# Two steps moved ahead in attention 1: the copy of sequence 2's normalised rows, and the projection of sequence 1's values

## The chip, the cores and the metric

The kernel runs on one core of a Trainium2 chip. The metric is the device time of one execution in microseconds (us). The core has engines that run side by side, each through its own list of instructions in order: PE (matmul, with PEld for its weight loads), DVE, ACT, POOL, and SP, which here only issues transfers (DMAs). They wait for each other through semaphores. A transfer is carried by 16 DMA engines; all transfers of this kernel are issued by SP on one queue.

## The reference

Two blocks of a transformer run over 8 sequences of 512 rows of 128 values: attention 0 (a linear attention), feed-forward 0 (with FP4 quantisation), attention 1 (causal softmax attention with 16 heads of 8), feed-forward 1 (a mixture of experts). Each is added to the input and has a normalisation ahead of it. The change touches the end of feed-forward 0 and the start of attention 1, which computes

```
def _L1_attn_ref(x, Wq, Wk, Wv, Wout):
    ...
    q = jnp.einsum('bld,dhe->blhe', x, Wq)
    k = jnp.einsum('bld,dhe->blhe', x, Wk)
    v = jnp.einsum('bld,dhe->blhe', x, Wv)
    a = jnp.einsum('bqhd,bkhd->bhqk', q, k) / Dh ** 0.5
    ...
    a = jnp.where(mask, a, NEG_INF)
    a = jax.nn.softmax(a, axis=-1)
    o = jnp.einsum('bhqk,bkhd->bqhd', a, v)
    return jnp.einsum('blhe,hed->bld', o, Wout)
x = x + _L1_attn_ref(_layernorm(x, axis=-1), L1_attn_Wq, L1_attn_Wk, L1_attn_Wv, L1_attn_Wout)
```

## The kernel before

The kernel is a row of four blocks, one after the other: `attention0`, `ffn0`, `attention1`, `ffn1`. Within a block each engine's work is written out in the order in which it runs; between two blocks all engines meet at a barrier (the branch at L858 is where they leave `ffn0`). Nothing reorders the instructions: the order of the text and the semaphores set everything.

**Attention 1** handles one sequence per period. A period has 20 steps (`STEPS`, four quads of heads with five units each). In a step of period i PE computes the scores of sequence i (`scores`, L1588), whose exponentials ACT takes (L1803) and POOL masks (L1865), and the scores of sequence i+1 once more in the other orientation (`maxima`, L1573 and L1577), from which DVE takes the row maxima (L1905, L1908, L1909, L1911). The two share three pairs of PSUM banks in turn (`ring`), so a matmul group waits until the group three places earlier was read. `weighted_v` (L1603) multiplies the exponentials with the values.

Ahead of period 0 stands the **opening**: 20 steps of `maxima` of sequence 0 alone, n = 0 to 19, in which a step n from 3 on waits until DVE has read unit n-3. Between these steps PE does small jobs that all use PSUM bank 0, so each waits for ACT's read of the one before:

- n = 0: `project_v(0, 0)` (L1630), the values of sequence 0; ACT keeps them (`keep_v`, L1778, semaphore `v_ready`);
- n = 2: `pr.turn_x(2)` (L782), which transposes the normalised rows of sequence 2. They are read from the buffer `xs`, into which SP copies them from `XN` (`pr.stage`, L754, semaphore `staged`). The copy is 256 KB;
- n = 4 and n = 6: `pr.project` (L787), the queries and keys of sequence 2; ACT keeps them (L798, `qf_ready`, `kf_ready`);
- n = 11: `turn_maxima(0, 0)` (L1637), which transposes the first half of the maxima of sequence 0, after DVE has split them (L1921 to L1924). ACT keeps them (L1784, `m_row`), and SP writes them to DRAM and back into `qS` (L1503, L1506). Period 0's first scores wait for that.

The values of sequence 1 are projected in period 0, step (1, 0), as those of each later sequence are in the period before their own. ACT keeps them there too.

**SP's part.** At the end of `ffn0` SP writes the split queries and keys of sequence 0 to DRAM (`parts_to_rows`, L763) and reads them back as rows of `qS` and `kS` (`pr.rows`, L777): 8 transfers of 192 KB. After the barrier its first transfer is `pr.stage(sp, 2)`, then the same two steps for sequence 1. `pr.stage(sp, n)` itself waits until `turn_x(n-1)` has read `xs`. ACT writes the normalised rows into `XN` in `norm_out` of `ffn0`, one sequence after the other, and counts them in `out_normed`.

## Time and profile before

| | us |
|---|---|
| median of 3 runs | 954.23 (954.03 to 956.84) |
| the profiled execution, its own time | 954.21 |
| its span, first to last instruction | 952.5 |
| end of `ffn0`, PE's first matmul of attention 1 | 378.11 |
| first scores of period 0 | 404.81 |

PE is busy for 872.2 us of the span, DVE for 737.9, ACT for 527.3, POOL for 453.6. The trace's instruction rows give the start, the duration, the engine, the line, and in brackets the idle time of the engine just before, with what ended it. "PEclk" or "granted clock" is the share of full speed that TensorE was given; 1.00 is 2.4 GHz and 0.50 is 1.2 GHz.

### The profile page before, as it was taken

To read this page: it belongs to the slowest core of one execution; us is meant where nothing else is said; L and a number is where in the kernel's file an instruction comes from. 1 tells how busy PE (TensorE), PEld (TensorE's weight loads), DVE (VectorE), ACT (ScalarE), POOL (GpSimd) and SP (SyncE) were. 2 spreads that over 40 slices of the span, in tenths; PEclk is the share of its full clock that TensorE was granted. 3 is DMA by queue.
4 is the path that set the end of the run, shared out by engine and by line. 5 is a ranking of instruction groups with operands and counts; after the bars stand their busy time and mean duration, and the time that the engine had idled before them with its cause. 6 is when DMAs were issued, how large, how long until landed. Compare 5 with 4: busy or idle time off the path is not lost. (4 is left out here: it accounts for less than half of the span.)

```text
span 952.5 us, 18274 instructions
## 1 busy us (share of the span) xinstructions
PE 872.2 (92%) x6457; PEld 577.6 (61%) x6457; DVE 737.9 (77%) x1496; ACT 527.3 (55%) x777; POOL 453.6 (48%) x599
## 2 busy tenths in 40 slices
PE   5999999998887777689999999998889999999997
PEld 4777777784665555344455454453557767766775
DVE  6888899878999995888888988987666646655542
ACT  4677778887465454267777777767523223222211
POOL 4123322324566665236566666456464355345344
PEclk9999999999999998779999999999999999999999
DMA  9200000000000007655445536200000000000000
GB/s 292 66 12 12 11 11 11 11 1 0 5 1 12 12 1 136 133 125 110 106 86 115 114 78 126 55 3 15 12 1 23 1 22 22 22 0 22 11 12 11
DMA packets 35641, 43.34 MB, mean 46 GB/s; under 512 B 4828, under 2 KB 27772, under 8 KB 35572
## 3 DMA queue, kind: packets, MB, share of 16 engines
q1 hardware_dynamic: 35569, 42.43, 18.6%
q8 instruction: 42, 0.69, 0.3%
q14 instruction: 30, 0.22, 0.1%
HBM read 21.21 MB, written 15.07 MB: 38 GB/s over the span
## 5 line engine op out<-in xcount | busy, mean ns | idle before, releaser
L1803 ACT ACTIVATE PT<-PS 128x1024 f32<-128x1024 f32 x160 | 162.7, 1023 | 56.5 <-PE PS L1588 56.2
L1865 POOL TENSOR_SCALAR_AFFINE_SELECT PT<-PT 128x256 f32<-128x256 f32 (+1 forms) x224 | 96.9, 448 | 109.6 <-ACT PT L1803 108.0
L2292 POOL TENSOR_TENSOR PRE_sb<-PRE_sb,VA 128x512 f32<-128x512 f32 x64 | 82.3, 1285 | 132.4 <-DVE PRE_sb L2360 132.3
L2258 ACT ACTIVATE sg_d<-PS 128x512 f32<-128x512 f32 x64 | 38.2, 597 | 160.0 <-PE PS L1326 160.0
L2360 DVE TENSOR_TENSOR PRE_sb<-sg_d,PS 128x512 f32<-128x512 f32 x64 | 44.0, 688 | 85.4 <-ACT sg_d L2258 84.7
L446 ACT ACTIVATE E<-PS,m 128x512 f32<-128x512 f32 x128 | 85.7, 687 | 36.8 <-PE PS L332 28.0
L1905 DVE TENSOR_REDUCE negm<-PS 128x2 f32<-128x1024 f32 x64 | 77.9, 1222 | 22.9 <-PE PS L1577 21.9
L1603 PE MATMUL PS<-PT,VA 128*32 128x512 f32 (+3 forms) x1024 | 89.5, 445 | 0.7 <-POOL PT L1865 0.7
L1573 PE MATMUL PS<-kS,qS 48*128 48x384 bf16 (+3 forms) x512 | 74.1, 314 | 8.1 <-ACT PT L1803 3.0
L491 POOL TENSOR_SCALAR Qs<-Qs 128x1024 f32<-128x1024 f32 x32 | 34.8, 1088 | 81.6 <-ACT Qs L427 81.0
L1908 DVE TENSOR_REDUCE negm<-PS 128x2 f32<-128x768 f32 x64 | 61.2, 957 | 12.8 <-PE PS L1577 11.5
L1588 PE MATMUL PS<-qS,kS 51*128 51x384 bf16 (+3 forms) x512 | 63.9, 308 | 2.9 <-DVE negm L1905 1.7
L360 PE MATMUL PS<-Qs,AW 128*128 128x512 f32 x128 | 59.2, 608 | 3.2 <-DVE PRE_sb L641 3.2
L1577 PEld LDWEIGHTS PS<-halves 64*128 64x128 bf16 x1024 | 48.9, 99 | 20.2 <-issue 2.9
L1588 PEld LDWEIGHTS PS<-qS,kS 51*128 51x128 bf16 x512 | 17.2, 94 | 69.6 <-issue 46.8
L1577 PE MATMUL PS<-halves 64*128 64x128 bf16 (+1 forms) x1024 | 58.8, 210 | 0.0
L422 ACT ACTIVATE Qs<-Qs,eps_c,ks 128x512 f32<-128x512 f32 x64 | 51.7, 814 | 0.0
L649 DVE SCALAR_TENSOR_TENSOR KB<-E,PS 128x512 f32<-128x512 f32 x64 | 42.3, 684 | 10.7 <-ACT E L446 9.0
L932 PE MATMUL PS<-low_space_sb,xT_sb 128*128 128x352 f32 x128 | 41.2, 465 | 9.1 <-DVE hh L1224 7.9
L670 DVE SCALAR_TENSOR_TENSOR Qs<-E,PS 128x512 f32<-128x512 f32 x64 | 42.6, 676 | 0.0
L664 DVE TENSOR_SCALAR E<-E 128x512 f32<-128x512 f32 x64 | 37.0, 579 | 6.8 <-ACT E L446 3.6
L2295 POOL TENSOR_TENSOR asum<-PRE_sb 128x512 f32<-128x512 f32 x32 | 41.0, 1282 | 2.5
(326 smaller groups left out, 2282.7 us busy)
## 6 DMA issues: line engine op xcount, KB each, us to landing
qk_rows<-parts SPq DMA_DIRECT2D x32, 192.0 KB, 2.8
qS<-qk_rows SPq DMA_DIRECT2D x32, 192.0 KB, 4.2
kS<-qk_rows SPq DMA_DIRECT2D x32, 192.0 KB, 4.6
xs_sb<-XN_sb SPq DMA_DIRECT2D x20, 256.0 KB, 2.3
qk_rows<-parts SPq DMA_DIRECT2D x32, 128.0 KB, 2.8
X_sb<-in_x_dram SPq DMA_DIRECT2D x8, 256.0 KB, 6.8
qk_rows<-parts SPq DMA_DIRECT2D x32, 64.0 KB, 2.5
out_dram<-X_sb SPq DMA_DIRECT2D x8, 256.0 KB, 2.3
```

Of the source, the lines that this page charges most:

```text
L360: ins = nc.tensor.matmul(PS[:, 6, :], AW[:, slot, c, :], Qs[:, slot, c, :], start=(c == 0), stop=(c == NC0 - 1))
L422: nc.scalar.activation(Qs[:, slot, c, :], Qs[:, slot, c, :], ACT.Ln, bias=eps_c[:, 0:1], scale=ks[:, c:c + 1]).then_inc(ln_ready, 1)
L446: nc.scalar.activation(E[:, u % RING, :], PS[:, RING_BANKS[u % RING], :], ACT.Exp, bias=m1[:, 0:1]).then_inc(e_ready, 1)
L1573: nc.tensor.matmul(bank[:, col:col + W], q[:, k * P:(k + 1) * P], key[:, 0:W], start=True, stop=False)
L1577: ins = nc.tensor.matmul(PS[:, 1 + 2 * ring_pair + j % 2, end - P + 64 * half:end], halves[rows, half, :], halves[rows, 2 + half, 64 * hal ...
L1588: ins = nc.tensor.matmul(PS[:, 1 + 2 * ring_pair + j % 2, col:col + W], key[:, kt * P:(kt + 1) * P], q[:, kt * P:S], start=True, stop=True)
L1603: ins = nc.tensor.matmul(PS[32 * j:32 * j + 32, 7, kt * P:S], VA[:, slot, kt, 4 * quad + j, :], PT[:, quad % 2, u, c:c + W], start=(kt == ...
L1803: nc.scalar.activation(PT[:, quad % 2, u, :], PS[:, b:b + 2, :].rearrange("p b n -> p (b n)"), ACT.Exp).then_inc(exp_ready, 1)
L1865: nc.gpsimd.affine_select(out=v, in_=v, pattern=[[0, 4 if u == 4 else 2], [1, P]], compare_op=ALU.is_ge, fill=0.0, base=0, channel_multipl ...
L1905: ins = nc.vector.tensor_reduce(negm[:, 3, :, 2 * quad + u], PS[:, b:b + 2, :], AX.X, ALU.max, negate=True)
L1908: nc.vector.tensor_reduce(negm[:, 2, :, pair], PS[:, b:b + 2, 0:384], AX.X, ALU.max, negate=True)
L2292: nc.gpsimd.tensor_tensor(acts[:, s, f, :], acts[:, s, f, :], W[:, slot, s, :], ALU.mult).then_inc(weighted, 1)
```

## The change

Four edits in three places:

- In `ffn0` SP issues `pr.stage(sp, 2)` after `pr.rows(sp, 0, 0, h)`, ahead of the barrier, behind a wait until `out_normed` is 3. In `attention1` the call is gone.
- In the opening PE projects the values of sequence 1 after step n = 8 (`project_v(1, 1)`), behind a wait for the kept keys of sequence 2 (`kf_ready` 3). ACT keeps the values there, behind the keys. `turn_maxima(0, 0)` at n = 11 now waits for these values (`v_ready` 2) instead of for the keys.
- In period 0 step (1, 0) has no projection of values any more, on PE and on ACT. The later periods keep theirs.
- In period 0 step (1, 3) `turn_ot(0, 0)` waits for `m_row` 2, where it waited for `v_ready` 2.

```diff
@@ ffn0, SP
             for h in range(NHALF):
                 pr.rows(sp, 0, 0, h)
-
+            sp.wait_ge(out_normed, 3)
+            pr.stage(sp, 2)
@@ attention1, SP
-            pr.stage(sp, 2)
             for m in range(2):
                 pr.parts_to_rows(sp, 1, 1, m)
@@ attention1, PE, period
-                    elif (quad, u) == (1, 0) and not (last or opens(i, 1)):
-                        if first:
-                            pe.wait_ge(m_row, 2)
-                        else:
-                            pe.wait_ge(o_normed, i * 4)
+                    elif (quad, u) == (1, 0) and not (first or last or opens(i, 1)):
+                        pe.wait_ge(o_normed, i * 4)
                         project_v(i + 1, 1 - slot)
...
                         if first:
-                            pe.wait_ge(v_ready, 2)
+                            pe.wait_ge(m_row, 2)
...
@@ attention1, PE, opening
+                elif n == 8:
+                    pe.wait_ge(kf_ready, 3)
+                    project_v(1, 1)
                 elif n == 11:
-                    pe.wait_ge(kf_ready, 3)
+                    pe.wait_ge(v_ready, 2)
                     pe.wait_ge(consts, 1)
                     turn_maxima(0, 0)
@@ attention1, ACT, period
-                    elif (quad, u) == ((1, 1) if opens(i, 1) else (1, 0)) and not last:
+                    elif (quad, u) == ((1, 1) if opens(i, 1) else (1, 0)) and not (first or last):
                         keep_v(i + 1, 1 - slot)
@@ attention1, ACT, opening
             pr.keep(act, 2, 1, k_ready, kf_ready)
+            keep_v(1, 1)
```

SP at the end of `ffn0`, before: the branches are the way out of `ffn0` and into `attention1`; L777 are the rows of sequence 0, L754 is the copy, L763 the parts of sequence 1.

```order
L777 DMA qS<-qk_rows 48x2048
L777 DMA kS<-qk_rows 48x2048
L858 UNCONDITIONAL_BRANCH
L1499 UNCONDITIONAL_BRANCH
L754 DMA xs_sb<-XN_sb 128x512
L763 DMA qk_rows<-parts 64x3x512
```

The same place after:

```order
L777 DMA qS<-qk_rows 48x2048
L777 DMA kS<-qk_rows 48x2048
L754 DMA xs_sb<-XN_sb 128x512
L858 UNCONDITIONAL_BRANCH
L1500 UNCONDITIONAL_BRANCH
L763 DMA qk_rows<-parts 64x3x512
```

The copy has moved ahead of the two branches, and still stands directly behind the last of the 8 row transfers, with no other transfer between them.

PE in the opening after, from the end of step n = 8 to step n = 9 (before, the L1630 row is not there and the others are the same):

```order
L1573 MATMUL PS<-kS,qS 128x128 x2
L1577 MATMUL PS<-halves 128x128 x2
L1577 MATMUL PS<-halves 128x64 x2
L1630 MATMUL PS<-wv1_sb,PRE_sb 128x128 x4
L1573 MATMUL PS<-kS,qS 128x256 x2
L1577 MATMUL PS<-halves 128x128 x2
```

PE in period 0, step (1, 0) and the start of step (1, 1), before:

```order
L1603 MATMUL PS<-PT,VA 32x512 x4
L1588 MATMUL PS<-qS,kS 128x512 x2
L1573 MATMUL PS<-kS,qS 128x512 x2
L1577 MATMUL PS<-halves 128x128 x2
L1577 MATMUL PS<-halves 128x64 x2
L1630 MATMUL PS<-wv1_sb,PRE_sb 128x128 x4
L1603 MATMUL PS<-PT,VA 32x384 x4
L1588 MATMUL PS<-qS,kS 128x512 x2
```

The same place after:

```order
L1603 MATMUL PS<-PT,VA 32x512 x4
L1588 MATMUL PS<-qS,kS 128x512 x2
L1573 MATMUL PS<-kS,qS 128x512 x2
L1577 MATMUL PS<-halves 128x128 x2
L1577 MATMUL PS<-halves 128x64 x2
L1603 MATMUL PS<-PT,VA 32x384 x4
L1588 MATMUL PS<-qS,kS 128x512 x2
```

The projection has left this place, and the weighted values (L1603) follow the maxima (L1577) directly.

## Rows read from the trace of the kernel before

**Rows 1.** The page's first part: busy us (share of the span), instructions.

```profile
PE 872.2 (92%) x6457; PEld 577.6 (61%) x6457; DVE 737.9 (77%) x1496; ACT 527.3 (55%) x777; POOL 453.6 (48%) x599
```

**Rows 2.** Timeline, PE, opening: start, us, engine, line, operation [idle before <-releaser].

```profile
384.13 0.63 PE L782 MATMUL PS<-ident_sb,xs_sb 128*128 128x128 f32 x4 [3.65 <-DMA xs_sb<-XN_sb]
...
390.71 0.25 PE L1577 MATMUL PS<-halves 64*128 64x128 bf16 x4
...
395.65 0.58 PE L1637 MATMUL PS<-identb,mpart 128*24 128x128 bf16 x4 [1.63 <-DVE mpart L1924]
```

**Rows 3.** Timeline, DVE, opening.

```profile
382.13 0.42 DVE L1909 TENSOR_REDUCE negm<-PS 128x2 f32<-128x256 f32 x1
385.38 0.96 DVE L1908 TENSOR_REDUCE negm<-PS 128x2 f32<-128x768 f32 x1 [2.83 <-PE PS L1577]
...
388.74 2.36 DVE L1905 TENSOR_REDUCE negm<-PS 128x2 f32<-128x1024 f32 x2 [0.94 <-PE PS L1577]
...
393.40 1.22 DVE L1911 TENSOR_REDUCE negm<-PS 128x4 f32<-128x1024 f32 x1
```

**Rows 4.** Timeline, ACT, opening.

```profile
380.60 0.60 ACT L1778 ACTIVATE VA<-PS 128x512 f32<-128x512 f32 x1
...
390.09 0.60 ACT L798 ACTIVATE PRE_sb<-PS 128x512 f32<-128x512 f32 x1 [1.37 <-PE PS L787]
```

**Rows 5.** Timeline, SP's queue, end of `ffn0` and opening: start and duration of the issue.

```profile
370.58 0.34 SPq L777 DMA_DIRECT2D qS<-qk_rows  x1
...
373.75 0.42 SPq L777 DMA_DIRECT2D kS<-qk_rows  x1
378.14 0.57 SPq L754 DMA_DIRECT2D xs_sb<-XN_sb  x1
...
393.99 0.42 SPq L777 DMA_DIRECT2D kS<-qk_rows  x1
396.88 0.30 SPq L1503 DMA_DIRECT2D max_rows<-mrow  x1
399.87 0.55 SPq L1506 DMA_DIRECT2D qS<-max_rows  x2
```

**Rows 6.** Transfers, KB, us from issue to landing: issued at 370.58, 373.75, 378.14.

```profile
qS<-qk_rows SPq DMA_DIRECT2D x1, 192.0 KB, 3.3
...
kS<-qk_rows SPq DMA_DIRECT2D x1, 192.0 KB, 8.4
...
xs_sb<-XN_sb SPq DMA_DIRECT2D x1, 256.0 KB, 5.9
```

**Rows 7.** Transfers, the same copy for sequence 0, issued at 330.38.

```profile
xs_sb<-XN_sb SPq DMA_DIRECT2D x1, 256.0 KB, 2.3
```

**Rows 8.** DMA queues, 380.8 to 384: packets, MB, share of 16 engines.

```profile
q8 instruction: 1, 0.02, 3.2%
```

**Rows 9.** Stretches: length, busy PE, PEld, DVE, ACT, POOL, clock, DMA share, GB/s.

```profile
372.00:381.00 9.00, 7.19 (x56) 5.23 (x54) 2.10 (x2) 6.21 (x12) 3.12 (x5) 0.84 1.04 173
...
382.40:383.60 1.20, 0.00 (x0) 0.00 (x0) 0.15 (x1) 0.03 (x1) 1.20 (x2) 1.00 0.06 14
...
385.00:388.40 3.40, 3.40 (x28) 1.37 (x24) 2.42 (x3) 0.67 (x2) 0.00 (x0) 0.51 0.95 203
...
395.40:415.80 20.40, 16.65 (x166) 8.16 (x168) 19.24 (x34) 8.54 (x11) 7.47 (x11) 0.50 0.73 153
...
409.10:415.40 6.30, 6.25 (x60) 2.89 (x60) 5.27 (x14) 3.61 (x4) 2.43 (x6) 0.50 0.91 200
```

**Rows 10.** Timeline, PE, period 0, step (1, 0).

```profile
416.20 1.16 PE L1630 MATMUL PS<-wv_sb,PRE_sb 128*128 128x128 f32 x8
417.29 0.85 PE L1603 MATMUL PS<-PT,VA 128*32 128x384 f32 x8
```

**Rows 11.** Timeline, DVE, after that step.

```profile
418.81 1.23 DVE L1905 TENSOR_REDUCE negm<-PS 128x2 f32<-128x1024 f32 x1 [1.27 <-PE PS L1577]
```

**Rows 12.** Timeline, ACT, after that step.

```profile
418.50 1.02 ACT L1803 ACTIVATE PT<-PS 128x1024 f32<-128x1024 f32 x1 [0.51 <-PE PS L1588]
```

## The prediction

> **What bounds the kernel now.** I first read the busy shares: PE has 872.2 us of work in a span of 952.5 us, 92% [rows 1]. So the kernel is bound by PE nearly everywhere, and a change gains only where PE's list gets shorter at a place where PE never waits, or where a wait of PE goes. The change touches two places, so I read the timeline engine by engine around each.
>
> In the opening of attention 1 PE does three steps and then stands for 3.65 us until the copy of sequence 2's rows has landed; its transposes start at 384.13 [rows 2]. This is the one long wait there. It passes to DVE, the engine that has the most work in the opening: it has read unit n = 2 by 382.55 (382.13 + 0.42), idles 2.83 us, then after the query projection another 0.94 us, and from 388.74 on runs without a pause [rows 3]. From there PE waits for DVE: 1.63 us before it transposes the split maxima at 395.65 [rows 2]. So in the opening DVE sets the pace, and a job added on PE there may cost nothing. In period 0 it is the other way round: at step (1, 0) PE has no idle time before its instructions [rows 10], while DVE idles 1.27 us and ACT 0.51 us until PE delivers [rows 11, 12].
>
> **The change part by part.** The sum is made against the profiled execution's own 954.21 us (the span and 1.7 us around it), which is within 0.02 us of the median, 954.23.
>
> *The copy, issued before the barrier.* SP issues the last row transfer at 373.75 (0.42 us), so the copy can be issued at about 374.2 instead of 378.14 [rows 5], 3.9 us earlier. Its two waits are for work that lies far back: `norm_out` is by then three sequences further than the third, and the transposes of sequence 1 have long read the buffer. SP otherwise only waits at the barrier until about 378, so the issue of 0.57 us delays nobody. The question is when the copy lands. The first of the 8 row transfers is issued at 370.58 and lands 3.3 us later, the last at 373.75 and lands 8.4 us later [rows 5, 6]: at 373.9 and 382.15. So 7 further transfers land in 8.25 us, one each 1.2 us, however fast SP issues them; it issued them within 3.2 us. They stand in line. The DMA engines were full from 372 to 381: share 1.04, 173 GB/s [rows 9]. The copy, issued at 378.14 and landing 5.9 us later, lands at 384.04, 1.9 us behind the last row transfer; the same copy with nothing ahead of it lands in 2.3 us [rows 6, 7]. It joined a line that lasted until 382.15, and stood directly behind the last row transfer. In the changed kernel it stands directly behind the same transfer, only longer. The line is as long, nothing that was behind the copy went ahead, and the last byte ahead of it moves when it did. So I take **0 us** for this move. It can't cost: rows for steps n = 10 on would have to be late by ten microseconds. Its other end is a landing before PE asks for it: then PE goes on when the values of sequence 0 are kept, at 381.20 (380.60 + 0.60) [rows 4], and DVE gets both idle times back, 2.83 + 0.94 = 3.77 us [rows 3]. I take the near end, because the row transfers show waiting in line directly.
>
> The Trainium skill (DMA: Bandwidth & Descriptors, Queues, rings and completion order) says that on each DMA engine descriptors are consumed in ring order. The landings one each 1.2 us agree with it; by that rule the earlier issue is worth nothing as long as the line never runs empty, and the whole change is worth the PE work alone. The same section says that completion is not in order per issuing engine; by that a gain up to the other end stays possible, and no row here shows it.
>
> What of the 1.9 us is not line? Once the share of the DMA engines has fallen, 0.06 is left from 382.4 to 383.6, that is one engine of 16 [rows 9], and in this stretch one instruction packet of another queue, which alone takes 3.2% of 16 engines over 3.2 us = 1.6 us of one engine, was carried [rows 8]. So a load of instructions held up one engine's part of the copy by about 1.2 to 1.4 us. It stays, since PE's and ACT's programs up to there are the same and reach it at the same time.
>
> *The projection of sequence 1's values, added after n = 8.* It takes 1.16 us at full clock [rows 10]. Step n = 8 ends at 390.96 (390.71 + 0.25), the keys are kept at 390.69 (390.09 + 0.60) [rows 2, 4], so PE starts it at once and ends near 392.1. Step n = 9 then starts near 392.1 and takes about 0.6 us, until 392.7. DVE takes that unit at 393.40 [rows 3]: 0.7 us to spare. Steps 10 and 11 wait for DVE as before. ACT's added 0.60 us falls into its idle time ahead of the maxima, and the new wait of `turn_maxima` (values kept near 392.8) is met 2.8 us before the split maxima are, near 395.6 [rows 2]. So **0 us**. The other end: if PE has the low clock there, the projection takes twice as long, 2.3 us, the cover of 0.7 us is used up and 0.5 us shows; uncovered altogether it would be 1.16 us.
>
> *The projection that period 0 no longer has.* The next instruction started at 417.29 against 416.20: **1.09 us** off a PE that never waits there [rows 10]. What would be late next? I followed the next steps with everything on PE 1.09 us earlier. DVE and ACT sat waiting for PE by 1.27 and 0.51 us [rows 11, 12]; ACT also loses its own 0.60 us keep there, and its next exponential was waiting for PE behind it. So both follow, DVE by the full 1.09 us, ACT likewise (0.51 + 0.60 = 1.11 us). The masks for the next weighted values are long done. After that each engine's distance to the others is as before, and since every later period is a chain of the same steps, the gain is carried to the end. Bounds: 0.5 us, if ACT followed by its idle time alone, and 1.16 us, the full duration.
>
> *The exchanged waits* at n = 11 and at (1, 3) are for things done microseconds earlier: 0 us.
>
> Sum: 0 + 0 - 1.09 = -1.1 us, 954.2 - 1.1 = **953.1 us**.
>
> **The rivals.**
>
> *A: as summed.* 953.1. To it belongs one variant of the clock. TensorE had 0.50 (1.2 GHz) from 395.4 to 415.8 [rows 9], after a stretch in which it mostly waited for DVE. The projection puts more matmuls ahead of that. Would the clock stay at 2.4 GHz, then little is won until 409, where DVE sets the pace, and of the 6.3 us from 409.1 to 415.4 no more than 6.3 - 5.27 = 1.0 us, since DVE is busy 5.27 us in it [rows 9]: 952.1. So A reaches from 951.9 to 954.3 with the spread of runs.
>
> *B: the copy lands early.* The line doesn't hold it, and PE's stall goes. For it: the copy has only 1.9 us of its own behind the line, and a stall of 3.65 us is the largest in the opening. Against it: the landings one each 1.2 us. Of the 3.77 us not all would last. Period 0 begins after the first half of the maxima went out to DRAM and back. SP sent them at 396.88 and could send them back in at 399.87, 3.0 us later; but it first issues rows of sequence 1 up to 394.41, and these hang on POOL's parts, not on the stall [rows 5]. So sending moves by 2.5 us at most and then stands behind the rows in line. Before, the way back had some 2 us to spare until 404.8. I take 3.3 us: 953.1 - 3.3 = 949.8, at most 949.3. A small relative: the copy lands before the load of instructions takes its engine, 1.3 us: 951.8.
>
> *C: slower, by the clock.* The low clock ended at 415.8, just before the projection of period 0 [rows 9, 10]. PE works without a pause there, and this mechanism takes the clock away for longer: dense f32 matmuls leave the place at which the clock had just come back, so it comes back later or falls again. The shortest low stretch of the opening is 3.4 us at 0.51 [rows 9]; PE at half speed loses half of it, 1.7 us: 953.1 + 1.7 = 954.8, and with two of them 956.5. It decides from 2.2 us of further low clock, which eat up the 1.09 us. Against it: the clock was back before the projection began, so what brought it back is still there. For it: the three runs of before already spread from 954.03 to 956.84.
>
> *D: the change doesn't do what it says.* The order of instructions shows that all four edits are there; the copy is issued earlier without landing earlier is A itself.
>
> **How the numbers follow.** A has a chance of 0.67, B 0.14, its relative at 951.8 0.06, C 0.13. The likeliest is A: 953.1. The range holds A, B and its relative and C's lower edge: 949.6 to 955.0. It leaves out the rest of C and the last bit of B, some 0.13. 0.3% is 2.9 us, about what a measurement of this kernel can tell from no change: faster means under 951.4, slower over 957.1. Faster is B with a little of the relative and of A's lower edge: 0.17. Slower by that much needs three low stretches: 0.03. Within: 0.80.
>
> **What would show it.** In the profile after: (1) the copy is issued near 374.2 and takes 9 to 10 us to land; PE's wait before the transposes is still 3 to 4 us and ends near 384. B is right if that wait is under 1 us and DVE's idle time of 2.83 us is gone. (2) L1630 stands near 391, DVE has no idle time before unit n = 9. (3) The first scores of period 0 start within 0.3 us of 404.8 after PE's start, measured from PE's first matmul: 26.7 us. (4) From step (1, 1) on everything is 1.1 us earlier than before. The prediction is wrong if the stall shrinks although the row transfers land as before, or if low-clock stretches lie elsewhere; then the clock's rows, not the steps, explain the difference.

## The result, and the profile after

| | before | after |
|---|---|---|
| median of 5 runs, us | 954.23 (952.78 to 956.84) | 949.82 (947.94 to 950.71) |
| ratio after / before, 95% interval | | 0.9949 [0.9931, 0.9966] |
| the profiled execution, its own time | 954.21 | 950.71 |
| its span | 952.5 | 949.0 |
| PE's first matmul of attention 1 | 378.11 | 378.33 |
| first scores of period 0 | 404.81 | 402.94 |

The change makes the kernel 4.4 us faster by these medians, where 1.1 us was predicted. A second series of 12 runs gave 0.9971 [0.9955, 0.9987] (below); over all 17 runs of after, and 72 of before in this and the next two series, the means are 951.1 and 954.5 us, 3.3 us apart. The forecast of 953.1 is wrong. The median came out where rival B (the copy lands early) had put it, 949.8; that is a coincidence, since the second series of the same kernel had 951.9 and what B described did not happen (below).

The page of after, first part: busy us (share of the span), instructions. It answers [rows 1].

```profile
PE 870.0 (92%) x6457; PEld 575.9 (61%) x6457; DVE 737.6 (78%) x1496; ACT 527.7 (56%) x777; POOL 454.0 (48%) x599
```

PE has 2.2 us less to do with the same number of instructions. No matmul was removed. The clock fits this: 1.2 GHz lasted 34 us of this execution and 42 us of the one of before (twice the span times what the mean granted clock, 0.982 and 0.978, lacks to 1). The prediction's sum has no term for it.

SP's queue of after, around the copy (start and duration of the issue), which answers [rows 5]:

```profile
371.60 0.34 SPq L777 DMA_DIRECT2D qS<-qk_rows  x1
...
374.76 0.42 SPq L777 DMA_DIRECT2D kS<-qk_rows  x1
375.31 0.57 SPq L754 DMA_DIRECT2D xs_sb<-XN_sb  x1
...
395.49 0.40 SPq L1504 DMA_DIRECT2D max_rows<-mrow  x1
400.22 0.55 SPq L1507 DMA_DIRECT2D qS<-max_rows  x2
```

Transfers of after, KB, us from issue to landing, for the last row transfer (issued at 374.76) and the copy (375.31), which answers [rows 6]:

```profile
xs_sb<-XN_sb SPq DMA_DIRECT2D x1, 256.0 KB, 7.9
kS<-qk_rows SPq DMA_DIRECT2D x1, 192.0 KB, 8.0
```

The row transfers are issued 1.0 us later than before, and the last one lands at 382.76. The copy lands at 383.21, **0.45 us behind it**. Before it landed at 384.04, 1.9 us behind the one at 382.15 [rows 6]. So the copy still stands in line behind the rows, but the tail of 1.9 us behind them has become one of 0.45 us.

PE's timeline of after in the opening (start, us, engine, line, operation, idle before and what ended it), which answers [rows 2]:

```profile
378.33 0.39 PE L1573 MATMUL PS<-kS,qS 48*128 48x512 bf16 x2 [2.40 <-DMA kS<-qk_rows]
...
378.80 2.07 PE L1630 MATMUL PS<-wv_sb,PRE_sb 128*128 128x128 f32 x8
...
383.39 0.63 PE L782 MATMUL PS<-ident_sb,xs_sb 128*128 128x128 f32 x4 [1.14 <-DMA xs_sb<-XN_sb]
...
384.84 1.13 PE L787 MATMUL PS<-PRE_sb,wq_sb 128*128 128x512 f32 x2
...
388.67 1.16 PE L1630 MATMUL PS<-wv_sb,PRE_sb 128*128 128x128 f32 x8
...
393.79 0.38 PE L1637 MATMUL PS<-identb,mpart 128*24 128x128 bf16 x4 [1.62 <-DVE mpart L1925]
...
402.94 0.60 PE L1588 MATMUL PS<-qS,kS 51*128 51x512 bf16 x2 [0.27 <-DVE negm L1910]
```

PE waits 1.14 us for the copy, not 3.65. Part of that is not the copy's doing: in this execution 1.2 GHz lay on PE's first 3.4 us, L1630 took 2.07 us instead of 1.16, and PE came to the wait later. In the second profile of this kernel (`after_again`), without that stretch, the wait is 2.74 us. The query projection (L787, `wq_sb`) takes 1.13 us; before, the low clock of 385.0 to 388.4 [rows 9] lay on it. The added projection of the values (L1630 at 388.67) takes 1.16 us. I cut the way from PE's first L1630 to the first scores into three: to the transposes 5.6 us before (from 378.5 to 384.13) and 4.59 after (378.80 to 383.39); from there to the split maxima 11.52 before (384.13 to 395.65) and 10.40 after; from there to the first scores 9.16 before and 9.15 after. So the opening is 2.1 us shorter, one half from the copy and the other half behind it, where the queries are projected. (The copy gained 1.4 us on the rows and only 1.0 on PE, because the rows landed 0.6 us later here and PE began 0.2 us later.)

DVE's timeline of after, which answers [rows 3]:

```profile
381.62 1.23 DVE L1906 TENSOR_REDUCE negm<-PS 128x2 f32<-128x1024 f32 x1 [1.48 <-PE PS L1577]
...
384.56 0.96 DVE L1909 TENSOR_REDUCE negm<-PS 128x2 f32<-128x768 f32 x1 [0.52 <-PE PS L1577]
...
386.90 2.35 DVE L1906 TENSOR_REDUCE negm<-PS 128x2 f32<-128x1024 f32 x2
389.16 0.95 DVE L1909 TENSOR_REDUCE negm<-PS 128x2 f32<-128x768 f32 x1
```

The idle times of 2.83 and 0.94 us [rows 3] have become 0.52 and none, and DVE runs through from 384.56, also across the added projection.

PE in period 0 of after, step (1, 0), where L1630 stood before [rows 10]:

```profile
411.69 1.56 PE L1603 MATMUL PS<-PT,VA 128*32 128x512 f32 x8
...
413.63 0.25 PE L1577 MATMUL PS<-halves 64*128 64x128 bf16 x4
413.81 0.85 PE L1603 MATMUL PS<-PT,VA 128*32 128x384 f32 x8
```

From the first scores to this L1603 (`128x384`) it is 10.87 us, and 12.48 before (404.81 to 417.29): 1.09 us are the projection. The other half microsecond goes with the clock, as the stretches of after show (length, busy PE, PEld, DVE, ACT, POOL, granted clock, DMA share, GB/s), which answer [rows 9]:

```profile
378.60:382.00 3.40, 3.40 (x30) 2.60 (x28) 1.61 (x2) 1.64 (x4) 1.08 (x1) 0.50 1.02 158
382.00:395.70 13.70, 9.59 (x137) 5.70 (x131) 13.04 (x19) 5.13 (x11) 2.58 (x3) 1.00 0.66 147
395.70:412.80 17.10, 13.33 (x136) 6.55 (x136) 16.08 (x30) 7.06 (x9) 7.17 (x11) 0.50 0.75 161
412.80:416.00 3.20, 3.20 (x44) 1.23 (x40) 3.06 (x6) 2.00 (x2) 1.02 (x3) 1.00 0.90 151
```

The long stretch at 0.50 (1.2 GHz) lasts 17.1 us instead of 20.4 and ends 1 us before this L1603, where before it ended 1.5 us before its own. (This half microsecond is not the change's. In a second profile of before, `before_again`, the low stretch lasts 17.1 us too, and the way takes 11.10 us; see the table at the end of the experiments.) The short one lies at PE's start, where PE waits for the copy afterwards anyway, and no longer on the queries. All of the rest is as long as before: both kernels take 231.7 us from here to the end of attention 1 and 303.5 us for `ffn1`. The sum: 2.1 (opening) + 1.6 (period 0) - 0.2 (PE's start 0.22 us later) = 3.5 us, the difference of the spans.

Two questions are left. Why does the copy land earlier behind the same row transfers? And how much of the gain is the copy's, the values', the clock's?

### The profile page after: what moved, and what is told of

It is laid out like the page before. It is cut to its first block and busy times, and to the rows that moved or that the text cites. A ratio compares the mean times of both kernels' runs of the same rounds, so it can differ in the third digit from the quotient of the medians.

```text
span 949.0 us, 18274 instructions
## 1 busy us (share of the span) xinstructions
PE 870.0 (92%) x6457; PEld 575.9 (61%) x6457; DVE 737.6 (78%) x1496; ACT 527.7 (56%) x777; POOL 454.0 (48%) x599
## 5 line engine op out<-in xcount | busy, mean ns | idle before, releaser
L2259 ACT ACTIVATE sg_d<-PS 128x512 f32<-128x512 f32 x64 | 38.3, 598 | 160.0 <-PE PS L1327 160.0
L1603 PE MATMUL PS<-PT,VA 128*32 128x512 f32 (+3 forms) x1024 | 89.1, 444 | 0.7 <-POOL PT L1866 0.7
L1577 PEld LDWEIGHTS PS<-halves 64*128 64x128 bf16 x1024 | 48.6, 98 | 19.8 <-issue 2.5
L1577 PE MATMUL PS<-halves 64*128 64x128 bf16 (+1 forms) x1024 | 58.2, 209 | 0.0
L933 PE MATMUL PS<-low_space_sb,xT_sb 128*128 128x352 f32 x128 | 44.4, 493 | 7.9 <-DVE hh L1225 6.7
L670 DVE SCALAR_TENSOR_TENSOR Qs<-E,PS 128x512 f32<-128x512 f32 x64 | 42.6, 675 | 0.0
L1573 PEld LDWEIGHTS PS<-kS,qS 48*128 48x128 bf16 x512 | 25.4, 96 | 28.3 <-ACT PT L1803 14.5
```

The lines of the kernel that those rows point to most:

```text
L1573: nc.tensor.matmul(bank[:, col:col + W], q[:, k * P:(k + 1) * P], key[:, 0:W], start=True, stop=False)
L1577: ins = nc.tensor.matmul(PS[:, 1 + 2 * ring_pair + j % 2, end - P + 64 * half:end], halves[rows, half, :], halves[rows, 2 + half, 64 * hal ...
L1603: ins = nc.tensor.matmul(PS[32 * j:32 * j + 32, 7, kt * P:S], VA[:, slot, kt, 4 * quad + j, :], PT[:, quad % 2, u, c:c + W], start=(kt == ...
```

## The experiments

All ratios are against the kernel before in the same series of runs.

### Each part alone, and both kernels again

`copy_only` moves the copy and nothing else:

```diff
@@ ffn0, SP
                 pr.rows(sp, 0, 0, h)
+            sp.wait_ge(out_normed, 3)
+            pr.stage(sp, 2)
@@ attention1, SP
-            pr.stage(sp, 2)
```

> Only the copy is moved ahead of the barrier; the values of sequence 1 stay in period 0. Theory L (the line alone: the copy lands when the row transfers ahead of it are through, wherever it is issued): the copy lands 1.0 to 1.9 us behind the last row transfer, the time is 0 to 1 us under that of the kernel before. Theory S (the copy's own issue time counts, the stall before the transposes shrinks): 2 to 3.5 us under it. In the profile: issue near 375, landing 8 us later; L has the copy's landing minus the last row transfer's landing at 1.9 us as before, S at 1.0 us.

`values_only` is the rest of the change, with the copy behind the barrier.

> Only the projection of sequence 1's values is moved into the opening; the copy is issued after the barrier as before. Both theories: 1.1 us under the kernel before, from step (1, 0) of period 0 on, no change in the opening. Theory V (the moved projection also changes the clock or the opening): 2 us or more under it, with a shorter low-clock stretch in period 0.

The two kernels again:

> The kernel before, unchanged, as a second profile of it and as the noise of these comparisons. Expected: ratio 1.000 within 0.002. Theory L says that what differed between the profiles of before and after beside the 1.1 us (the place of the low-clock stretches, and whether the load of instructions falls on the copy) differs between executions of the same kernel too; then this profile has its low stretches elsewhere than the first, and opening and landing move with them.

> The changed kernel, unchanged, second profile. Expected 4.4 us under the kernel before (950 us). If the gain in the opening belongs to the change (theory S), DVE's idle time in the opening is again near 2 us in place of 4 us and the copy lands about 1.0 us behind the last row transfer; if it was the luck of one execution (theory L), one of them is not there.

Measured, 12 runs each: `copy_only` 954.75 us, 1.0003 [0.9986, 1.0020]; `values_only` 952.47, 0.9984 [0.9970, 0.9998]; `before_again` 955.01, 1.0005 [0.9992, 1.0019]; `after_again` 951.94, 0.9971 [0.9955, 0.9987]. The values are worth 1.8 us by means [0.9, 2.6], with the predicted 1.1 inside. `after_again` is 2.7 us under before by means [1.6, 3.8], less than the 4.4 expected. The copy alone shows nothing in the total, as theory L had it. But its profile shows the earlier landing, as theory S had it. PE's timeline of `copy_only`:

```profile
380.55 0.63 PE L782 MATMUL PS<-ident_sb,xs_sb 128*128 128x128 f32 x4 [2.71 <-DMA xs_sb<-XN_sb]
...
382.00 1.13 PE L787 MATMUL PS<-PRE_sb,wq_sb 128*128 128x512 f32 x2
```

and the same two rows of `values_only`, whose copy is issued behind the barrier:

```profile
381.90 0.63 PE L782 MATMUL PS<-ident_sb,xs_sb 128*128 128x128 f32 x4 [4.16 <-DMA xs_sb<-XN_sb]
...
383.85 2.07 PE L787 MATMUL PS<-PRE_sb,wq_sb 128*128 128x512 f32 x2
```

The wait is 1.45 us shorter with the copy moved, at nearly the same start of attention 1 (PE's first matmul at 375.47 and 375.37), and the queries are projected at full clock.

### Why the copy lands earlier

Three kernels vary when it is issued. `copy_ahead` is after with the copy issued some 20 us before the row transfers, `copy_ahead_only` the same without the values:

```diff
@@ ffn0, SP, ahead of the parts of sequence 0
+            sp.wait_ge(out_normed, 3)
+            pr.stage(sp, 2)
             for m in range(2):
                 pr.parts_to_rows(sp, 0, 0, m)
```

> The changed kernel, but SP issues the copy of sequence 2 right after the ones of sequences 0 and 1 (near 349 us), ahead of the parts and rows of sequence 0, when the queue is empty. Both theories agree that the copy has then landed long before PE asks; PE's wait before the transposes ends when ACT has kept the values of sequence 0 (about 3.1 us after PE's first matmul), DVE's idle time in the opening falls from 4 us (before) and 2 us (after) to under 1 us. The opening, from PE's first matmul to the first scores of period 0, was 26.7 us before and 24.6 after: 23.0 to 23.6 expected. Time: 4 to 4.5 us under the kernel before. If the way of the maxima through DRAM becomes the bound instead, the opening stays at 24 or more and the first scores wait for a transfer.

> The kernel before, with nothing but the copy moved to near 349 us; the values of sequence 1 stay in period 0. Opening as in the kernel with both (23.0 to 23.6 us), 3 to 3.4 us under the kernel before in all. If copy and values do not add up (theory V, a shift of the low-clock stretches eats the copy's gain when the values stay), it is less than 1.5 us under it.

`copy_late` is after, but SP waits before the copy, still in `ffn0`, until four row transfers have landed:

```diff
             sp.wait_ge(out_normed, 3)
+            sp.wait_ge(pr.rows_in[0], 64)
             pr.stage(sp, 2)
```

> The changed kernel, but SP issues the copy only when the first four row transfers have landed, about 6.9 us after the first was issued (as late as in the kernel before), still in front of the barrier. Theory Q (the place in line relative to the load of instructions decides: issued as late as before, the load stands ahead of the copy on one DMA engine again): the copy ends about 2.5 us behind the last row packet, as before, the opening takes 26 to 26.7 us, and of the change only the 1.1 us of the values stay. Theory B (being issued before the barrier decides): the copy ends 1.15 us behind the last row packet, opening 24.6 us, 3 us under the kernel before.

Measured: `copy_ahead` 950.52 us, 0.9957 [0.9941, 0.9973]; `copy_ahead_only` 951.02, 0.9959 [0.9945, 0.9974]; `copy_late` 951.86, 0.9979 [0.9964, 0.9994]. The copy alone again, in the same series, 12 runs:

> The kernel with only the copy moved, again: its profile had an opening 2.0 us shorter than the kernel before, but its timed runs showed no gain (1.0003, 0.9986 to 1.002). If the opening's gain is real and the first timing was unlucky in the low-clock stretches, now 0.996 to 0.9995 and an opening of 24.6 us; if something later takes it back, 1.000 again with an opening of 24.6 us.

954.74 us, 1.0003 [0.9989, 1.0018].

`copy_late` decides the question of the line. SP's queue:

```profile
376.26 0.42 SPq L777 DMA_DIRECT2D kS<-qk_rows  x1
379.72 0.57 SPq L754 DMA_DIRECT2D xs_sb<-XN_sb  x1
```

and its PE:

```profile
380.98 0.39 PE L1574 MATMUL PS<-kS,qS 48*128 48x512 bf16 x2 [2.37 <-PEq L858]
...
384.99 0.63 PE L782 MATMUL PS<-ident_sb,xs_sb 128*128 128x128 f32 x4 [1.63 <-DMA xs_sb<-XN_sb]
...
386.44 1.12 PE L787 MATMUL PS<-PRE_sb,wq_sb 128*128 128x512 f32 x2
```

The copy is issued 3.5 us after the last row transfer (before: 4.4 us [rows 5]), and yet it lands 0.6 us behind that transfer (384.85 and 384.22), not 1.9, and PE waits 1.63 us for it, not 3.65. It is still issued ahead of the barrier (PE leaves `ffn0` behind it, at L858); SP's wait also holds the barrier up, so that PE starts 4.7 us after the last row transfer was issued and not 3.6 as in after, which is why the waits are less telling than the landings. So the 3.9 us of earlier issue are not what brings the gain. Something that comes behind the barrier stood ahead of the copy in before. The queues show it. Before, 380.8 to 382.2, the one packet of instructions is there with the copy's:

```profile
q1 hardware_dynamic: 122, 0.21, 87.1%
q8 instruction: 1, 0.02, 7.3%
```

and then, 382.2 to 383.7, only 10 of SP's packets are left, one after the other on one engine; the first line is the share of the 16 engines in 40 slices, in tenths:

```profile
DMA  0000003000003000003000020001010100100000
...
q1 hardware_dynamic: 10, 0.02, 5.0%
```

In after, 382.6 to 384.2, SP's packets end at once and the instructions come behind them:

```profile
DMA  9400000000000000000000000000000000000000
...
q8 instruction: 1, 0.02, 4.3%
q1 hardware_dynamic: 14, 0.01, 1.4%
```

The load of instructions (7.3% of 16 engines over 1.4 us = 1.6 us of one engine) was carried ahead of the copy's packets on one engine, and the copy's last ones came that much late: in before and the three other profiles that issue the copy behind the barrier and have no fillers, its last packet ended 2.43 to 2.69 us behind the last packet of the rows, 2.54 on average. With the copy issued ahead of the barrier it is 1.02 to 1.24 us in eight profiles, 1.14 on average, and the instructions begin within 0.15 us of the copy's end. The copy gains **1.4 us** by going ahead of a load of instructions, with rows and line as they were; by the landings it is 1.3 us (1.8 and 0.5 us behind the rows on average). What no trace shows is when the load was asked for. That the barrier decides is read from the order that came out in these twelve profiles. In `fill_before` (below), whose copy is issued behind the barrier too, the load began just after the copy's first packets, and the last one ended 1.67 us behind the rows.

`copy_ahead` shows the other end, a copy that has landed long ago. PE's timeline:

```profile
379.84 0.39 PE L1574 MATMUL PS<-kS,qS 48*128 48x512 bf16 x2 [1.35 <-DMA kS<-qk_rows]
382.36 0.66 PE L782 MATMUL PS<-ident_sb,xs_sb 128*128 128x128 f32 x4
...
402.84 0.61 PE L1589 MATMUL PS<-qS,kS 51*128 51x512 bf16 x2 [0.53 <-DMA qS<-max_rows]
```

No wait is left before the transposes, and the first scores now wait for the maxima's way through DRAM (0.53 us), the give-back of which rival B spoke. By means of 7 and 12 runs, `copy_ahead` is 1.2 us under after (950.6 and 951.8, of different series), which is within their spread.

`copy_ahead_only`, where the values stay in period 0, is 3.5 us under before by means [2.1, 4.7], as expected. So a copy that has landed long before it is wanted shows in the timed runs without any help from the values, and is worth about the 3.3 us that rival B gave to such a copy. The values add 0.3 us [-1.4, 2.0] to it. `copy_late` is 2.0 us under before [0.8, 2.9], where 3 were expected, with 6 runs.

### Does the copy alone shorten the opening each time?

Three more profiles of `copy_only` and one of before, a single execution each:

> Only the copy moved, one more profiled execution. Its timed runs fall into two groups, 950 to 953 us with 34 to 38 us at the low clock, and 954.7 to 957 us with 42 to 53 us. Theory K (the clock takes the gain back): a profile of the second group has the opening 2 us shorter as the others, and more low-clock stretches than the kernel before, in period 0 or after, that cost 4 us. Theory O: in the second group the opening itself is as long as before (26.3 us), with the copy landing late.

> As copy_look_1: the same kernel, to catch an execution of the second group. K: opening 23.6 to 24.3 us, extra low stretches elsewhere. O: opening 26.3 us.

> As copy_look_1: the same kernel, to catch an execution of the second group. K: opening 23.6 to 24.3 us, extra low stretches elsewhere. O: opening 26.3 us.

> The kernel before, one more profiled execution, for the same question from the other side: where the executions at 954 to 957 us have their low-clock stretches. Expected under K: opening 26.2 to 26.8 us with the copy 2.5 us behind the last row packet in every execution, and the difference between executions in the number and place of low stretches alone.

They took 950.73, 954.16, 955.55 and 958.33 us. PE's waits for the copy are 3.06, 3.03 and 2.63 us, and 4.41 in before. But in `copy_look_3` low clock lies where it costs time. Two of its stretches:

```profile
382.30:389.10 6.80, 6.06 (x43) 3.13 (x43) 3.21 (x5) 1.20 (x3) 1.63 (x2) 0.50 0.70 148
...
696.30:703.20 6.90, 6.08 (x14) 3.92 (x14) 1.27 (x2) 0.59 (x2) 3.80 (x3) 0.51 0.00 0
```

1.2 GHz lay on the queries (2.08 us), and again at the start of `ffn1`, where PE works without a pause: `ffn1` took 306.2 us there against 303.5.

### With fillers against the low clock in the opening

Four kernels carry the same filler matmuls (bf16, 128x512, into PSUM bank 7, whose results nothing reads), so that PE is busy where it used to wait. The four are before, the copy alone, after, and `copy_ahead`.

```diff
+            def fill(k):
+                for _ in range(k):
+                    nc.tensor.matmul(PS[:, 7, :], halves[:, 0, :], halves[:, :, :].rearrange("p a n -> p (a n)"), start=True, stop=True)
...
+                if n >= 9:
+                    fill(2)
                 if n >= 3:
                     pe.wait_ge(max_read, n - 2)
...
+                    fill(8)
                     pe.wait_ge(v_ready, 1)
                     pr.turn_x(pe, 2)
...
+                    fill(6)
                     turn_maxima(0, 0)
...
+                    if first and step < 4:
+                        fill(2)
                     wait_banks(n)
                     scores(i, slot, quad, u, ring(n))
```

> The kernel before with filler matmuls (128x512, bf16, into PSUM bank 7, their results are used by nothing): 8 ahead of the transposes of sequence 2, 2 ahead of each opening step from n = 9, 6 ahead of turn_maxima, 2 ahead of each of the first four steps of period 0. They are meant to keep TensorE's granted clock at 1.00 through the opening, in all four kernels alike. It is the base for the other three. If the low clock of the opening and of period 0's start (34 to 38 us per execution at the least, at half speed) goes in part, it is up to 3 us faster than the kernel before; if the clock stays as it was, the fillers cost up to their own time, 42 of 0.21 us at full clock, 9 us, less what falls into waits: +2 to +5 us.

> The same fillers with the copy's earlier issue alone. Theory T (the copy's gain is real, and the low-clock stretches behind it take it back in the timed runs): with the clock held it is 1.3 us under fill_before (the copy's earlier landing; the query projection is at full clock in both). Rival U (the 1.35 us of the copy's landing is off the path to the end, given back at the maxima's trip through DRAM): 0 +- 0.4 us against fill_before, and the stretch from the values of sequence 0 to the first scores is as long in both profiles.

> The same fillers with both parts of the change. T: 2.4 us under fill_before (1.3 from the copy, 1.1 from the values). U: 1.1 us under it. A third theory V (the change's excess over 1.1 us comes from less low clock, not from the copy): 1.1 us under it too, and the low clock is as long in fill_before and fill_after.

> The same fillers with the values moved and the copy issued near 349 us, long before it is wanted. T: all of the 3.65 us wait is gone: 3 to 4 us under fill_before. U and V: 1.1 us under it.

Stretches of `fill_before`, the opening and where the long low stretch used to be:

```profile
378.00:395.00 17.00, 14.58 (x150) 7.24 (x150) 13.58 (x19) 6.11 (x11) 4.30 (x4) 1.00 0.84 165
395.30:415.80 20.50, 17.83 (x221) 8.29 (x222) 19.61 (x34) 9.79 (x13) 9.15 (x15) 1.00 0.71 145
```

The 0.50 of [rows 9] is 1.00. Over the 12 timed runs (a run's low time is twice its span times what its mean clock lacks to 1) 1.2 GHz lasted 20.5 us in `fill_before` and 17 to 19 us in the others, and 43 us in before. Medians: 952.43 us (0.9987 [0.9969, 1.0005]), 950.12 (0.9963 [0.9949, 0.9978]), 949.76 (0.9959 [0.9943, 0.9974]) and 950.03 (0.9955 [0.9941, 0.9969]). By means, `fill_copy` is **2.3 us [1.0, 3.8] under `fill_before`**: the copy alone has an effect with the opening's low clock gone. The 1.3 us expected are inside the interval, and the rival's 0 is excluded. The two were not quite alike in clock: `fill_copy` had 3.4 us less of 1.2 GHz per run, about 1 us of time by the slope of 0.28 given at the end (an estimate). The profiles of this pair, both at 1.00 from the first L1630 to the L1603 of step (1, 0), give the cleaner size. PE's waits for the copy, `fill_before` and then `fill_copy`:

```profile
383.76 0.63 PE L782 MATMUL PS<-ident_sb,xs_sb 128*128 128x128 f32 x4 [1.67 <-DMA xs_sb<-XN_sb]
...
381.97 0.63 PE L782 MATMUL PS<-ident_sb,xs_sb 128*128 128x128 f32 x4 [0.73 <-DMA xs_sb<-XN_sb]
```

The wait is 0.94 us shorter, the opening takes 25.04 and 24.09 us, and period 0 up to that L1603 takes 10.65 us in both: the copy brings 0.95 us, and nothing is given back. (In this `fill_before` the load of instructions had delayed the copy by less than in before, as said above.)

The values show 0.4 us [-0.8, 1.5] on top (`fill_after` against `fill_copy`); 1.1 is inside, so the timed runs can't size them; in the profiles period 0 up to L1603 takes 9.54 instead of 10.65 us, the 1.1. `fill_ahead` adds nothing to that (0.1 us [-1.2, 1.1]), where 1 to 2 us more were expected; the eight fillers ahead of the transposes now stand where the wait was, so it says little on the wait. No version here is clearly faster than after.

### With fillers at the start of ffn1

`ffn1` is not touched by the change, but in its first sequence PE waits 2.23 and then 1.35 us for DVE, and behind that a short low stretch follows. Where it falls decides its price. In ten of the 20 profiles it starts 43.0 to 44.6 us after ACT's last `mrow` row, and `ffn1` takes 303.2 to 303.5 us, as in the one profile of before that has no such stretch; in eight it starts 48.7 to 49.9 us after that row, and `ffn1` takes 304.9 to 306.2. In before it lies on the step between the two waits, and DVE is waited for again behind it:

```profile
692.22 0.79 PE L1324 MATMUL PS<-xTl_d,w1h 128*128 128x512 f32 x1 [2.23 <-DVE PRE_sb L2360]
...
698.50 0.48 PE L1324 MATMUL PS<-xTl_d,w1h 128*128 128x512 f32 x1 [1.35 <-DVE PRE_sb L2360]
```

In `copy_only` the step between them ran at full clock, PE waited 2.91 us, and the low stretch lay behind, with no wait to hide it:

```profile
693.41 0.72 PE L1325 MATMUL PS<-xTl_d,w1h 128*128 128x512 f32 x1 [2.91 <-DVE PRE_sb L2360]
```

The stretches of `copy_only` there, from the first wait's end to the second's and behind it:

```profile
687.10:693.40 6.30, 3.39 (x16) 2.41 (x17) 5.83 (x15) 1.06 (x2) 2.67 (x3) 1.00 0.00 0
693.50:696.90 3.40, 3.40 (x9) 2.64 (x9) 0.36 (x1) 0.00 (x0) 3.32 (x3) 0.50 0.00 0
```

From one wait's end to the other's it is 6.3 us in both, so the first place costs nothing; `ffn1` as a whole took 303.47 us in before and 305.04 in `copy_only`. Two kernels have fillers at these two waits only:

```diff
+                    if first and n == 4:
+                        pe.wait_ge(ex.lg_ready, i + 2)
+                        fill(0, 9)
                     if first and n == 5:
                         pe.wait_ge(att_added, NB)
+                        fill(1, 6)
                     hidden(i, slot, n)
```

> The kernel before with filler matmuls in the first sequence of feed-forward 1 only (22x512, bf16, 9 ahead of step n = 4 and 6 ahead of step n = 5; nothing uses their results), where PE waits 2.23 and 1.35 us for DVE and a stretch of low clock has followed in every profile but one. The base for the next one: within 0.5 us of the kernel before, if the stretch goes; up to 1 us slower if it stays.

> The same fillers with the copy's earlier issue alone. Theory T2 (the copy's 1.3 to 1.9 us are taken back by the low stretch at the start of feed-forward 1, which in three of five profiles fell behind the waits and cost 1.5 us and more): 1 to 2 us under late_fill_before. Rival W (that stretch falls on either kernel by chance; what is lost is lost in period 0, where the low clock lies under more dense work when it begins 13.6 us after PE's start instead of 17): 0 +- 0.7 us against late_fill_before.

Measured: 953.76 us (1.0003 [0.9985, 1.0021]) and 952.93 (0.9984 [0.9970, 0.9999]); by means the copy is worth 1.5 us here, with an interval [0.0, 3.1] that just reaches zero. The fillers did not always hold the clock: `late_fill_before` has a low stretch behind them,

```profile
696.80:700.20 3.40, 3.40 (x10) 2.62 (x9) 0.15 (x1) 0.00 (x0) 3.32 (x3) 0.50 0.00 0
```

and its `ffn1` took 305.0 us. So this pair leans to the theory of the low stretch in `ffn1` (T2) and doesn't settle it.

### What the profiles add up to

For each profile: PE's wait for the copy, the query projection, the opening (first L1630 to first scores), and from there to the L1603 of step (1, 0), and `ffn1` (last `mrow` row of ACT to the end). All from timeline rows, in us.

| | wait | queries | opening | period 0 to L1603 | both | `ffn1` |
|---|---|---|---|---|---|---|
| before | 3.65 | 2.07 | 26.3 | 12.5 | 38.8 | 303.5 |
| before_again | 4.02 | 2.07 | 26.6 | 11.1 | 37.7 | 303.5 |
| before_look_1 | 4.41 | 1.70 | 27.0 | 12.2 | 39.2 | 305.1 |
| values_only | 4.16 | 2.07 | 26.8 | 11.4 | 38.1 | 303.5 |
| copy_only | 2.71 | 1.13 | 24.3 | 12.1 | 36.3 | 305.0 |
| copy_only_again | 1.63 | 1.12 | 23.6 | 12.1 | 35.7 | 303.4 |
| copy_look_1 | 3.06 | 1.12 | 24.6 | 11.9 | 36.5 | 305.0 |
| copy_look_2 | 3.03 | 1.75 | 25.3 | 13.1 | 38.3 | 303.4 |
| copy_look_3 | 2.63 | 2.08 | 26.1 | 11.4 | 37.5 | 306.2 |
| after | 1.14 | 1.13 | 24.1 | 10.9 | 35.0 | 303.5 |
| after_again | 2.74 | 1.13 | 24.3 | 10.8 | 35.1 | 303.5 |
| copy_late | 1.63 | 1.12 | 23.2 | 10.9 | 34.1 | 303.2 |
| copy_ahead_only | 0 | 1.13 | 23.9 | 11.8 | 35.6 | 305.0 |
| copy_ahead | 0 | 1.13 | 22.6 | 10.0 | 32.6 | 304.9 |
| fill_before | 1.67 | 1.13 | 25.0 | 10.7 | 35.7 | 303.5 |
| fill_copy | 0.73 | 1.13 | 24.1 | 10.7 | 34.7 | 303.5 |
| fill_after | 0 | 1.13 | 24.7 | 9.5 | 34.3 | 303.5 |
| fill_ahead | 0 | 1.13 | 26.0 | 9.5 | 35.5 | 304.9 |
| late_fill_before | 4.23 | 1.97 | 26.9 | 12.3 | 39.2 | 305.0 |
| late_fill_copy | 2.94 | 1.12 | 24.5 | 12.0 | 36.5 | 304.5 |

The column "both" is 38.6 us on average in the three of before, 36.9 in the five with the copy alone, 35.1 in the two of after. So the copy brings 1.7 us and the whole change 3.5 us, against 3.3 us between the timed means. For the full change, profile and timing agree. Split by the two columns, the full change has 2.4 us in the opening (26.6 and 24.2) and 1.1 us in period 0 (11.9 and 10.8, the predicted 1.09): the half microsecond more of the first pair of profiles was chance. For the copy alone profile and timing don't quite agree: pooled with `copy_only_again` 24 timed runs stand 0.2 us [-0.8, 1.1] under before. `ffn1` gives 0.6 us of the 1.7 back in these profiles (304.6 against 304.0 on average), and the two filler pairs show 2.3 and 1.5 us where part of the clock's play is taken out. That the copy's gain is real is shown by `fill_copy` and, for a copy issued 20 us earlier still, by `copy_ahead_only`. That low stretches take it back when it stands alone is not shown. The costly place in `ffn1` came up in four of seven profiles with the copy moved and the values in place (without `late_fill_copy`), in two of seven with the values moved, and in two of five with neither moved, too few to tie it to the change. One more thing differs: in the profiles of the copy alone the long low stretch starts 13.5 to 13.8 us after the first L1630 in three of five and lasts 20.4 us, and in the two of after it starts at 16.9 and 17.0 us and lasts 17.1 us. But `before_again` has 17.3 and 17.1 us, and `copy_ahead` 13.6 and 17.1, so this is no clear mark of either kernel. In the timed runs 1.2 GHz lasts 43 us per run on average in the copy alone, 42.6 in before, 40 in `values_only`, and 39 in `after_again`.

## Why the prediction was wrong

- **The copy, taken at 0 us: the step that failed.** "The line is as long, nothing that was behind the copy went ahead" is right, as the landings of after and `copy_late` show. The next step is wrong: the load of instructions, "it stays, since PE's and ACT's programs up to there are the same and reach it at the same time". It does come at about the same time, but which of the two goes first on the engine that they share is not fixed by that: with the copy issued ahead of the barrier, the load came behind it in all eight profiles, with the copy issued behind the barrier ahead of it in all four. I had counted 1.2 to 1.4 us for it myself, and had even named the case (B's relative, 951.8, 0.06), but as a thing that would need the copy to *land* earlier; it only needs to be *queued* earlier. Measured: 1.4 us, near the 1.3 of that relative. The rule on ring order in the Trainium skill (DMA: Bandwidth & Descriptors, Queues, rings and completion order) speaks of one ring. Here SP's queue and the queue of instructions wanted the same engine, and in these traces the copy went first when it was issued ahead of the barrier, and the load when it was not; that is what decided here.
- **What the shorter wait does to the clock: left out.** The prediction has the clock as a danger (C) and as a variant behind 395.4. It did not ask what a shorter wait does to the 0.51 stretch on the queries right behind that wait [rows 9]. The queries take 1.13 instead of 2.07 us, 0.94 us less in after, and they take 1.12 or 1.13 in every profile with the copy moved but two, where all five profiles without the move and without fillers in the opening have 1.70 to 2.07. This is the second half of the opening's gain. That the shorter wait keeps the clock up is what these profiles suggest; it is not shown, and `copy_look_3` had 2.08 us behind a wait of 2.63.
- **The values added in the opening, 0 us: right.** From the transposes to the split maxima nothing was added; DVE has no idle time from 384.56 on. The prediction put L1630 near 391; it came at 388.67, since all was earlier.
- **The values removed in period 0, 1.09 us: right.** It is 1.1 us on the table's averages and in the filler pair. The 0.5 us more of the first pair of profiles lies within the variant at 952.1 that was given, but a second profile of before has it as well.
- **Exchanged waits, 0 us: right.** PE waits 1.62 us for the split maxima, 1.63 before.
- **The signs named ahead.** (1) did not come: the copy took 7.9 us to land, not 9 to 10, and PE waited 1.14 us (2.74 in the second profile), not 3 to 4. (3) did not come: from PE's first matmul to the first scores it is 24.6 us (378.33 to 402.94), not 26.7. (2) held for DVE. (4) did not come in size: from step (1, 1) on everything is earlier by the same amount, but by 3.5 us instead of 1.1. The prediction's own sign of being wrong (the stall shrinks although the rows land as before, or low stretches lie elsewhere) came in both its parts.
- **Rival B**, 949.8, had the size of the first series by luck, and not the way. It let the whole stall of 3.65 us go by an early landing. In fact 1.4 us went by the place in line (1.0 of it on PE in this profile), 0.9 by the clock on the queries, 1.1 by the values and, in this pair of profiles, 0.5 by the end of the low stretch; and the give-back at the maxima's way through DRAM, which B counted, shows only in `copy_ahead`.
- **Rival C** (slower by the clock) did not come: low time fell from 42 to 39 us per run.

The range 949.6 to 955.0 held the median of this result, barely, and the chance of 0.06 for B's relative, the rival that had the load of instructions in it, was too low: the argument "they stand in line" was taken to cover the 1.9 us that I had found *not* to be line.

## What to carry to other kernels

When a transfer lands later than its line explains, ask what shares its engines in that moment, and whether it was queued before or after. Here a load of instructions came in each profile 2.5 to 4.7 us after PE's first matmul behind the barrier, so the transfer wanted there was better issued ahead of the barrier, and better still 20 us ahead of that, where it lands in 2.3 us. A wait on PE can cost more than its own length if a low clock follows it: price the matmuls behind it at both clocks. And a gain of 1 to 2 us that the profiles show on average may not show in 24 timed runs while low stretches of 3.4 us come and go; fillers that keep the clock up in both kernels can bring it out. One pair of profiles is not enough to split a gain: a second profile of each kernel showed which half microsecond was chance.

## What the runs showed of the hardware that was not expected

- A load of instructions of 16 KB (one packet of the instruction queue) held one DMA engine for 1.4 to 1.6 us while the rows and the copy were under way (1.1 us in after, behind them) and delayed the landing of a 256 KB copy on 16 engines by 1.3 to 1.4 us: in before the copy's last eight packets ended one after the other from 382.68 to 383.56, behind the load's end at 382.46, where all its others had ended by 382.23.
- Executions of one kernel differ by where the low clock falls: before ran from 951.7 to 956.7 us in one series of 35, and with 34 to 38 us at 1.2 GHz it took 951.7 to 952.5, with 42 us around 954. The straight line through all 125 runs of before in the four later series has 0.28 us of time per us of low clock.
- A short low stretch of 3.4 us in `ffn1` cost nothing or 1.5 us, by whether it fell before or behind a wait for DVE, in 18 profiles.
- Filler matmuls kept 1.00 where 0.50 had lasted 20.4 us, and low time fell from 43 to 20 us per run; the kernel before gained 1.5 us [0.3, 2.8] by doing more work.
